# A four-layer graph network on one core: the order of TensorE's work in the edge stages

## The reference

```python
x = _layernorm(x + _L0_gnn_ref(x, node_vec1, edge_attr_4, edge_attr_8, ..., src, dst), axis=-1)
x = _layernorm(x + _L1_gnn_ref(x, node_vec1, src, dst, edge_attr_4, edge_attr_10, ...), axis=-1)
x = _layernorm(x + _L2_gnn_ref(x, node_vec1, edge_attr_16, edge_attr_4, src, dst, ...), axis=-1)
x = _layernorm(x + _L3_gnn_ref(x, ..., edge_attr_4, edge_attr_10, src, dst, ...), axis=-1)
```

```python
weight = jax.nn.silu(edge_length_embedded @ W_fc1) @ W_fc2
gs = x1s[edge_src]          # rows of the source nodes after a linear map
gv = x1v[edge_src]
mid0a = w0 * gs * e_s
mid0b = w3 * (jnp.einsum('euc,ec->eu', gv, e_v) / SQRT3)
mid1a = w1[:, :, None] * gs[:, :, None] * e_v[:, None, :]
mid1b = w2[:, :, None] * gv * e_s[:, :, None]
agg = jax.ops.segment_sum(edge_feat, edge_dst, num_segments=n) / np.sqrt(NUM_NEIGHBORS)
```

## Time and profile before

| | |
|---|---|
| median of 3 runs | 4588.22 us |
| profiled execution | 4606.82 us, span 4605.1 us, granted clock 0.902 |
| TensorE busy | 3557.9 us, 77% |
| VectorE, GpSimd, ScalarE busy | 59%, 52%, 47% |
| chain that ended last | PE 37%, another core or an unknown queue 18%, ACT 13%, issue 13%, DVE 12% |

### The profile page before, as it was taken

How to read it: one execution, slowest core, us unless ns; L and a number is a source line. 1 busy time by engine, 2 the same in 40 slices (tenths; PEclk the granted TensorE clock), 3 DMA queues, 4 the chain that set the end, 5 groups by cost and what they waited for, 6 DMA issues and landing times.

```text
span 4605.1 us, 99292 instructions
## 1 busy us (share of the span) xinstructions
PE 3557.9 (77%) x23534; PEld 3169.8 (69%) x23534; DVE 2735.3 (59%) x11380; ACT 2167.5 (47%) x5622; POOL 2414.6 (52%) x2869
## 2 busy tenths in 40 slices
PE   3677778566577777889967777789987887787887
PEld 2677767566576777777756666677766777777776
DVE  3455555788644444578844444458865555555887
ACT  0223223566422222367733333347764444445888
POOL 1555555788555555466645555530015555555776
PEclk9788888888888888899978888989989999999999
DMA  9411122777411111278821111238861111113776
GB/s 355 157 42 43 45 47 60 233 252 255 129 32 39 42 42 42 53 249 291 289 57 37 40 43 42 47 117 298 298 193 31 34 40 41 40 43 128 259 261 231
DMA packets 424040, 572.49 MB, mean 124 GB/s; under 512 B 219010, under 2 KB 242340, under 8 KB 419618
## 3 DMA queue, kind: packets, MB, share of 16 engines
q1 hardware_dynamic: 295170, 322.46, 23.2%
q0 software_dynamic: 81680, 114.98, 9.8%
q10 hardware_dynamic: 47088, 133.90, 7.4%
HBM read 356.10 MB, written 233.79 MB: 128 GB/s over the span
## 4 chain that ended last, share of the span: by engine, by line
PE 37%; another core or an unknown queue 18%; ACT 13%; issue 13%; DVE 12%; DMA 4%; ACTq 2%; DVEq 1%; POOL 0%; SPq 0%; POOLq 0%
PE bank L799 7%; ACT arena L1071 5%; PE bank L830 4%; PE bank L828 4%; PE bank L838 3%; PE bank L806 3%; DVE stats L1425 3%; PE bank L852 3%; PE bank L829 2%; PE bank L787 2%; ACT nT L1045 2%; DVE arena L1418 1%; PE bank L907 1%; DVE mv L1436 1%
## 5 line engine op out<-in xcount | busy, mean ns | idle before, releaser
L584 POOL DMA_INDIRECT aggregates<-arena,meta x784 | 798.9, 1019 | 1083.4 <-ACT arena L993 344.1
L1071 ACT ACTIVATE arena<-arena,shift,rstd 128x160 f32<-128x160 f32 x1600 | 697.2, 508 | 64.9 <-DVE shift L1356 63.0
L571 POOL DMA_INDIRECT xg<-x_after,meta x588 | 584.3, 994 | 264.7 <-issue 258.4
L799 PE MATMUL bank<-same_all,msg 128*128 (+1 forms) x4704 | 644.6, 291 | 1.2 <-issue 1.2
L799 PEld LDWEIGHTS bank<-same_all,msg 128*128 128x128 f32 x4704 | 615.6, 209 | 1.7 <-issue 0.4
L1272 DVE SCALAR_TENSOR_TENSOR carry<-carry,meta,bank 128x3 f32<-128x3 f32 x784 | 170.7, 218 | 669.1 <-ACT arena L978 402.6
L978 ACT ACTIVATE arena<-bank 128x381 f32<-128x381 f32 x784 | 368.5, 492 | 357.9 <-remote 199.2
L828 PE MATMUL bank<-w,arena 128*128 128x98 f32 (+1 forms) x1568 | 373.7, 324 | 179.7 <-issue 89.2
L806 PE MATMUL bank<-nT,weights 128*128 128x128 f32 x1176 | 230.4, 308 | 345.2 <-ACT nT L972 269.5
L828 PEld LDWEIGHTS bank<-w,arena 128*128 128x128 f32 x1568 | 297.0, 218 | 283.7 <-issue 231.7
L1425 DVE BATCH_NORM_STATS2 stats<-arena 128x6 f32<-128x160 f32 x1600 | 453.5, 314 | 41.9 <-DVE arena L1418 10.0
(11 more groups left out here) (169 smaller groups left out, 7842.9 us busy)
## 6 DMA issues: line engine op xcount, KB each, us to landing
arena<-aggregates SPq DMA_DIRECT2D x400, 324.0 KB
x_after<-arena ACTq DMA_DIRECT2D x300, 320.0 KB
arena<-x_after SPq DMA_DIRECT2D x300, 320.0 KB
aggregates<-arena ACTq DMA_DIRECT2D x25, 1296.0 KB
arena<-nodes SPq DMA_DIRECT2D x100, 320.0 KB
out<-arena SPq DMA_DIRECT2D x100, 320.0 KB
same_all<-sorted_dst SPq DMA_DIRECT2D x7, 1792.0 KB, 13.3
aggregates<-arena,meta POOLq DMA_INDIRECT x784
```

What stands on the lines that cost most here:

```text
L571: gp.indirect_dma_start(xg[:, k % XGR, 4 + t * F:4 + (t + 1) * F], None, xtab[l], at).then_inc(gathered[k], 16)
L584: gp.indirect_dma_start(agg, at, tot[:, kk % TRING, t, 0:AW], None, bounds_check=NP - 1, oob_is_err=False).then_inc(spread[kk], 16)
L799: last = nc.tensor.matmul(bank[5 + t][:, c * P:(c + 1) * P], sent[:, c * P:(c + 1) * P], same_all[:, bass.ds(here[t], P)], start=True, sto ...
L1071: last = nc.scalar.activation(row, row, ACT.Identity, bias=shift[:, kk, t:t + 1], scale=rstd[:, kk, t:t + 1])
```

## The change

The change spreads each pair over five of TensorE's iterations instead of three. TensorE's order for q becomes: T(q), fc2(q-1), w1(q-1), S(q-3), fc1(q), M0(q-4), M1(q-4). ScalarE's becomes: L972(q), in layer 3 L1011(q-1), L978(q-3) twice, L983(q), totals of q-4. VectorE mends q-2, behind the messages of q; and it waits before it overwrites `msg` until the sums of q-2 are done. In layer 3 the adding of the two groups' totals (L1255) is for q-4 instead of q-3. `aggT` has two buffers. GpSimd's and SyncE's programs stay as they are. TensorE and ScalarE run 102 iterations per stage instead of 100, VectorE 100 instead of 99 (102 instead of 101 in layer 3).

The core of TensorE's part (the calls that are left out only move with their lag):

```diff
-        o1, o2, o3, o4 = 512, 512 + 4 * 384, 512 + 4 * 384 + 4 * F, 512 + 4 * 384 + 4 * F + 2 * MC
+        o1, o2, o3, o4 = 512, 512 + 4 * 384, 512 + 4 * 384 + 4 * F, 512 + 4 * 384 + 4 * F + 4 * MC
-        aggT = arena[:, o3:o4].rearrange("p (t h e) -> p t h e", t=2, h=3)
+        aggT = arena[:, o3:o4].rearrange("p (b t h e) -> p b t h e", b=2, t=2, h=3)
...
+                    if made:
+                        k1 = (k - 1) % 2
+                        pe.wait_ge(h_act, edge_count(l, q - 1))
+                        wait(pe, wy_ready, edge_count(l, q - 2))
...
+                        last.then_inc(w_ready, 1)
+                        pe.wait_ge(turned_out, edge_count(l, q - 1))
+                        if G == 1:
+                            wait(pe, f_free, edge_count(l, q - 2))
...
+                        else:
+                            wait(pe, f_summed, q - 1)
...
+                        last.then_inc(f_ready, 1)
+                    if sent:
...
+                        pe.wait_ge(msg_ready, edge_count(l, q - 3))
...
+                            wait(pe, summed_out[t], edge_count(l, q - 4))
+                            wait(pe, mended[t], edge_count(l, q - 4))
...
+                    def second_map(t):
+                        pe.wait_ge(summed_out[t], edge_count(l, q - 4))
+                        pe.wait_ge(mended[t], edge_count(l, q - 4))
...
+                            if t == 0:
+                                wait(pe, tot_out[1], edge_count(l, q - 5))
+                            else:
+                                pe.wait_ge(tot_out[0], edge_count(l, q - 4))
...
+                    if given:
                         pe.wait_ge(turned_out, edge_count(l, q))
                         wait(pe, h_act, edge_count(l, q - 1))
...
-                    if has_old:
+                    if mapped:
                         second_map(0)
-                    if has_new:
-                        pe.wait_ge(h_act, edge_count(l, q))
...
-                    if has_old:
                         second_map(1)
-                steps(pe, 0, NPAIR + 2, EDGE_STEADY, edge_products)
+                steps(pe, 0, NPAIR + 4, EDGE_STEADY, edge_products)
```

ScalarE's totals and VectorE's message part:

```diff
                     def totals(t):
-                        kk, tt = back(k, turn, 2)
-                        act.wait_ge(tot_ready[t], edge_count(l, q - 2))
-                        if t == 0 and (l or within(q, 6, NPAIR + 6)):
-                            k6, t6 = back(k, turn, 6)
-                            wait(act, spread[k6], slot_count(l, k6, t6) * 32)
+                        kk, tt = back(k, turn, 4)
+                        act.wait_ge(tot_ready[t], edge_count(l, q - 4))
+                        if t == 0 and (l or within(q, 8, NPAIR + 8)):
+                            wait(act, spread[k], slot_count(l, k, turn - 1) * 32)
...
                     nc.vector.tensor_tensor(dprod[:, :, :, :], wy[:, k2, :, 1:4, S:96], fv, ALU.mult).then_inc(dprod_ready, 1)
+                    for t in range(2):
+                        wait(dve, summed[t], edge_count(l, q - 2))
+                    alone(dve, passed["dve"])
...
-                    if within(q, 1, NPAIR):
-                        mend(0)
-                        mend(1)
                     dve.wait_ge(dprod_ready, edge_count(l, q))
                     nc.vector.tensor_reduce(msg[:, k2, :, 0, S:MF], dprod[:, :, :, :].rearrange("p t d v -> p t v d"),
                                             AX.X, ALU.add).then_inc(msg_ready, 1)
-
-                steps(dve, 0, NPAIR + (3 if l == 3 else 1), EDGE_STEADY if l else FIRST_STEADY, edge_vectors)
+                    if within(q, 2, NPAIR):
+                        mend(0)
+                        mend(1)
+
+                steps(dve, 0, NPAIR + (4 if l == 3 else 2), EDGE_STEADY if l else FIRST_STEADY, edge_vectors)
```

More of the change, by code:

```diff
@@ L776, in edge_products @@
                     k2 = k % 2
[L777 to L781, removed]
-                    if has_new:
+                    given, made = within(q, 0, NPAIR), within(q, 1, NPAIR + 1)
+                    sent, mapped = within(q, 3, NPAIR + 3), within(q, 4, NPAIR + 4)
+                    if given:
                         pe.wait_ge(gathered[k], slot_count(l, k, turn) * 32)
@@ L833, in edge_products @@
-                    if has_new:
-                        if G == 1:
-                            wait(pe, f_free, edge_count(l, q - 1))
-                            for c in range(3):
-                                a, e = c * CH, min((c + 1) * CH, W1C)
-                                last = nc.tensor.matmul(bank[3][:, a:e], xT[:, k2, c * P:(c + 1) * P], w1[l][:, a:e],
-                                                        start=True, stop=True)
-                        else:
-                            wait(pe, f_summed, q)
-                            both = lambda ap, a, e: ap.rearrange("p (g c) -> p g c", g=2)[:, :, a:e]
-                            for c, t, a, e in ((0, 0, 0, 128), (1, 0, 128, 160), (1, 1, 0, 96), (2, 1, 96, 160)):
-                                last = nc.tensor.matmul(both(bank[3 + t][:, 0:2 * F], a, e), xT[:, k2, c * P:(c + 1) * P],
-                                                        both(w1[l], t * F + a, t * F + e), start=True, stop=True)
-                        last.then_inc(f_ready, 1)
@@ L847, in edge_products @@
-                    if has_old:
-                        second_map(0)
-                    if has_new:
-                        pe.wait_ge(h_act, edge_count(l, q))
-                        if PACKED[l]:
-                            last = nc.tensor.matmul(bank[2][:, 0:384], hT[:, k2, 0:P], fc2[l], start=True, stop=True)
-                        else:
-                            for t in range(2):
-                                last = nc.tensor.matmul(bank[2][:, t * 192:(t + 1) * 192], hT[:, k2, t * P:(t + 1) * P],
-                                                        fc2[l], start=True, stop=True)
-                        last.then_inc(w_ready, 1)
@@ L968, in edge_copies @@
                             clear(run)
-                    if has_new:
+                    if within(q, 0, NPAIR):
                         act.wait_ge(turned, edge_count(l, q))
@@ new lines, in edge_copies @@
+                        last.then_inc(fa_out, 1)
+                    if within(q, 3, NPAIR + 3):
+                        for t in range(2):
+                            act.wait_ge(summed[t], edge_count(l, q - 3))
+                            wait(act, tot_ready[t], edge_count(l, q - 5))
+                            sums = bank[5 + t][:, 0:MC].rearrange("p (h e) -> p h e", h=3)
+                            nc.scalar.activation(aggT[:, (k - 3) % 2, t, :, 1:P], sums[:, :, 1:P], ACT.Copy).then_inc(summed_out[t], 1)
```

119 lines of the change are left out of this document (59 added, 60 removed).

## The result

The changed kernel takes 4682 us against 4588 us, a ratio of 1.021 (95% interval 1.0175 to 1.0245). Forecast were 4180 us, so the sign was wrong, and rival (C), 4670 us with a chance of 0.09, is what happened. The profiled execution took 4705.6 us, 4703.9 of them the span, 98.8 us longer than before.

A forecast was written before the change was run, and what follows sets the result against it. TensorE was taken as the bound, stopped by late-seen completions and a lowered clock. Layers 0 to 2 save 444 us, layer 3 adds 25, ends 12: 407 us off 4588 gives 4181, said as 4180; range 4000 to 4490 us.

The forecast's parts named there:

- (C): Rival: layer 3's bare copy between M0 and M1 costs 0.65 to 1.6 us a pair; layers 0-2 gain 0; 4670 us, chance 0.09.
- T to fc1: TensorE's stop before fc1, layers 0 to 2: more work covers it, 1.09 us a pair in layer 1 falls to 0.27.
- The other stops: TensorE's idle time not before fc1 (fc1 to fc2, S to M0, features to w1): 0.65 us a pair in layer 1 becomes 0.1.
- (D): Rival: another wait in the same iteration replaces each one removed, layer 3 even; within 0.2% of 4588 us, chance 0.04.
- (B): Rival: completions get later with GpSimd's load, VectorE's new wait and mends stall; layers 0-2 at 6.7 us a pair; 4455 us, chance 0.22.
- VectorE's added wait: Layers 0 to 2: VectorE's wait for S(q-2) before overwriting messages adds 0.3 us a pair, bounds 0 and 3.6.
- GpSimd: Loop through GpSimd takes 15.1 us over three pairs, 5.0 a pair, floor 5.2; does not stop a pair of 5.9.
- Clock: TensorE's granted clock in layers 0 to 2 rises from 0.87 to 0.94, making busy time about 5.1 us a pair.
- Layer 3: Bare wait of M1 for M0's copy adds 0.65 us a pair, other stops save 0.4: 7.90 becomes 8.15 us, bounds 7.3 and 8.9.
- Ends: Stage ends: two more short iterations with bare handoffs cost 3 us a stage (0 to 9), 12 us more in all.
- (A): Rival: GpSimd becomes the bound, layers 0 to 2 fall to 5.2 us a pair, layer 3 to 7.3; 3890 us, chance 0.13.

The follow-up runs named there:

- The edit of the run's length: Changed kernel with one more GpSimd gather a pair in layer 1, gathers as plain SyncE loads in layer 2: 8.18 and 4.53 us a pair.
- the kernel with one edit per layer: Changed kernel: layer 0 unaltered, layer 1 one more gather, layer 2 gathers as plain loads, layer 3 M0 ahead of S; 4366 us beside 4530.
- group 2: Runs with late completions: changed kernel unaltered 4605 us, ratio 1.015 to the kernel before; both kernels also with three GpSimd fills a pair, 4331 us (before) and 4406 us (changed).
- the kernel before with the pause: Kernel before with three GpSimd fills of an unused tile behind each pair's scatters, completions late: 4331 us, ratio 0.955.
- group 1: Runs with completions on time, kernel before 3776 us: fc2 between M0 and M1 in layer 3, old order in layer 3, plain loads in both kernels; 3665 to 3935 us.
- group 5: Runs with late completions, kernel before 4530 us: changed kernel with another edit in each of layers 1 to 3, layer 0 as control; 4366 us.

## Why the prediction was wrong

By its own steps:

- *T to fc1.* Right: 0.27 us a pair was forecast, 0.23 to 0.27 measured.
- *The other stops.* Wrong: fc2 and T took up 1.26 us a pair in layer 0 against 0.1 in sum. The time went where it was not looked for, as (D) and (B) say, since the period did not shrink.
- *VectorE's added wait.* Over-sized, and harmless. In layer 1 L1327 waits 76.2/84 = 0.9 us a pair, but w1 behind it has 0.0 us of idle time; TensorE paid nothing of the 0.3 there.
- *GpSimd.* **The step that failed.** I laid the loop through GpSimd over three pairs and spread 3 us of lateness over it, 5.0 us a pair. But the lateness isn't a sum to be spread: most of it starts inside a run and ends just behind it, and the next run waits for a completion that is held so. The period is then that of one run and what follows it, 4.9 us and 2.15 us to the next start (mean of layer 1). The edit of the run's length shows this dependence; that the loop closes through the totals alone is argued. The pieces stood in rows 5 and 6: 202 us of GpSimd's waiting for L993, and a copy 1.1 us behind the last gather. I used them for (C) and then gave it 0.09.
- *Clock.* 0.94 forecast, 0.82 to 0.85 measured in layers 0 to 2, and with it 5.1 us of busy time a pair against 5.5 to 5.7 (423.37/77 in layer 0, 478.38/84 in layer 1). It was derived from stops that were to vanish; they moved. The Trainium skill (TensorE: Matmul & The Clock Gate, HAM oscillation) has long idle gaps as the cause, and the runs agree: 1.00 in layer 2 of the kernel with one edit per layer, where the stops went, 0.80 in its layer 1, where they grew.
- *Layer 3.* +0.65 - 0.4 forecast, +1.47 measured. The mechanism and the bare price (0.59 with completions on time) were right. Wrong was to leave the lateness out of it: M0's completion is now late in nearly every round, so before M1 stand 175.4/69.5 = 2.5 us instead of 1.75. And the clock fell: TensorE's idle time went from 1.6 to 2.5 us a pair, but its busy time also from 516.92/82.3 = 6.3 to 477.77/69.5 = 6.9, at 0.86 against 0.94, for which the forecast had nothing.
- *Ends.* 12 us forecast, 10 left over in the first measurement, some 39 in group 2, and 25 over three stages in the other state if the kernel before stands at 5.2 us there.

(C) had the right place, the right round and the right condition ("if layers 0 to 2 gain less than 0.2 us a pair"; they gained 0.19 on the mean, 0.41 in group 2, and layer 3 lost 1.5). It came to 4670 with 0 us gained and 70 lost where 55 and 144 were measured; that the two errors nearly cancel is luck. (B)'s picture, lateness that grows as TensorE gets faster, is what the completions show (over pairs 16 to 95 they come on the mean 2.0, 1.9 and 2.2 us behind the recorded end in layers 0 to 2 against 1.4, 1.3 and 1.3 before). Whether they bind by themselves, beside GpSimd's wait, stays open. (A) would have needed completions on time, and even then layer 3's M0 to M1 stood against it.

Of the versions run, the changed kernel with M0 ahead of S beats the kernel before by 0.5% where completions are on time. Where they are late its layer 3 gives back 1.07 x 98 = 105 us of the changed kernel's, which from 4605 us makes 4500 against 4539, an estimate. There the kernel before with the pause is the fastest measured, at 4331 us. No version beat both kernels in both states by a measurement.

## What to carry to other kernels

If an engine waits, every round, for the same handoff, close the loop through that engine before costing anything else, and ask whether its own work delays the signal that it waits for; here one more gather on that engine lengthened the period by its full size, and reordering another engine shortened it by 0.04 to 0.59 us. A cover that is moved to one handoff is taken from another: M0 and M1 side by side were bare, and each handoff in the new order must be costed with the latest completion that the trace shows, not with the clean one. And where a wait's length is the same for a light and a heavy round, ask whether it is a delay tied to an event before counting it as slack.

## What was not expected of the hardware

- TensorE's completions are late or punctual by the group of runs, and not by the chip: the same chip had the kernel before at 3776 us in group 1 and at 4530 us in group 5. About nine in ten of the late ones end, by the record, inside a run of GpSimd's indirect DMAs or within 0.3 us of its end. In layers 0 to 2 of the changed kernel 75 to 80 of 100 late ones come through behind the end of a run, at a median of 1.3 to 1.5 us (0.65 us with the short runs of layer 2 in group 5); the others come through inside one. But such a run is not enough: with completions on time GpSimd runs indirect DMAs for over 100 us without a pause (layer 0, M0 ahead of S), and of 620 completions there 608 end inside the run and none is late. What decides between the two states was not found, and it is worth 20% of this kernel.
- A pause of 1.5 us on the busiest queue made the kernel 4.5% faster in one state and 15% slower (with M0 early) in the other. Whether a shorter pause, or one between gathers and scatters, gains more where completions are late, and what the changed order in layers 0 to 2 alone is worth there as a whole, was not measured.
